# Merging four stages of a per-image pipeline into two software-pipelined loops, with one intermediate sent through DRAM

## The reference

```
x = gamma * (softmax(max(x x^T) - x x^T) x) + x        # channel attention: a 64 x 64 matrix per image
x = conv_long(x, filters of layer 1) + x * bias1       # 256-long causal filters along H and W
y = haar2d(x); for i in 0, 1: f = einsum(y * v[i], conv_w[i]); acc += sign(f) * relu(|f| - tau[i])
x = haar2d_inverse(acc) + x                            # wavelet shrinkage
x = conv_long(x, filters of layer 3) + x * bias3
```

## Time and profile before

| | before |
|---|---|
| median of 3 runs | 6840.18 us (6823.84 to 6842.23) |
| the profiled execution | 6835.24 us, of which the span from first to last instruction is 6833.4 us |
| TensorE clock granted, mean | 0.974 of full |
| PE busy | 6388.9 us |
| DVE / ACT / POOL busy | 4433.1 / 3968.3 / 2698.2 us |
| bytes over DMA | 944.27 MB |

### The profile page before, as it was taken

One profiled execution on the slowest core, in us unless ns is written; L12 is line 12 of the kernel. 1 busy time (PEld: TensorE's weight loads), 2 busy tenths in 40 slices (PEclk: granted clock), 3 DMA queues, 4 the chain that ended last, 5 costly groups with the idle time before them and its releaser, 6 DMA issues.

```text
span 6833.4 us, 144168 instructions
## 1 busy us (share of the span) xinstructions
PE 6388.9 (93%) x41056; PEld 5800.8 (85%) x41056; DVE 4433.1 (65%) x7037; ACT 3968.3 (58%) x5913; POOL 2698.2 (39%) x2052
## 2 busy tenths in 40 slices
PE   8998999889998899988999889998899988999689
PEld 7987999779997799977999779997799977998579
DVE  3667646676566764677646776567765677656766
ACT  1568545675456754567545775457654576545865
POOL 0149311483115831167311673117631176311852
PEclk9999999999999999999999999999999999999999
DMA  6654666546664466644666446664466644665236
GB/s 222 126 139 138 123 168 132 141 129 130 169 132 141 126 130 167 132 146 122 131 167 132 147 121 131 167 132 145 122 130 169 131 149 119 131 173 125 80 86 129
DMA packets 621293, 944.27 MB, mean 138 GB/s; under 512 B 62358, under 2 KB 456759, under 8 KB 621208
## 3 DMA queue, kind: packets, MB, share of 16 engines
q1 hardware_dynamic: 547480, 808.74, 51.3%
q10 hardware_dynamic: 73728, 134.25, 5.3%
HBM read 673.92 MB, written 268.83 MB: 138 GB/s over the span
## 4 chain that ended last, share of the span: by engine, by line
PE 75%; DVE 10%; ACT 8%; issue 3%; DMA 2%; POOL 1%; DVEq 1%; SPq 0%; ACTq 0%; POOLq 0%
PE ps L359 26%; PE ps L361 13%; PE ps L387 7%; PE ps L379 7%; PE ps L464 7%; PE ps L416 7%; PE ps L370 6%; DVE work L767 4%; DVE ps L782 4%; ACT ps L601 4%; ACT mag L598 4%; DMA work<-in_x_pix 1%; POOL mag L844 1%; PE ps L337 1%; DMA coef<-work 0%
## 5 line engine op out<-in xcount | busy, mean ns | idle before, releaser
L359 PE MATMUL ps<-work 128*128 128x256 f32 x8192 | 2455.2, 382 | 23.9 <-POOL work L833 16.3
L361 PEld LDWEIGHTS ps<-work 128*128 128x128 f32 x8192 | 1561.8, 191 | 214.3
L361 PE MATMUL ps<-work 128*128 128x128 f32 x8192 | 1578.0, 274 | 0.0
L359 PEld LDWEIGHTS ps<-work 128*128 128x128 f32 x8192 | 1315.8, 192 | 121.5 <-issue 20.7
L833 POOL COPY work<-field 128x512 f32 (+1 forms) x512 | 312.8, 614 | 2308.6 <-DVE ps L731 1623.3
L844 POOL TENSOR_TENSOR mag<-mag,sgn 128x1024 f32<-128x1024 f32 x512 | 1091.8, 2132 | 331.9 <-ACT mag L598 315.6
L862 POOL TENSOR_TENSOR split_a<-field,split_a 128x512 fp32r<-128x512 f32 x512 | 650.8, 1271 | 1418.8 <-ACT split_a L616 1418.8
L782 DVE TENSOR_TENSOR ps<-ps,tau_t 128x1024 f32<-128x1024 f32 x512 | 631.2, 1233 | 313.0 <-ACT ps L601 313.0
L569 ACT ACTIVATE work<-ps 128x512 f32<-128x512 f32 x512 | 306.1, 598 | 874.0 <-PE ps L361 871.1
L616 ACT ACTIVATE split_a<-field 128x512 fp32r (+1 forms) x512 | 322.9, 631 | 698.9 <-PE ps L379 694.6
L767 DVE TENSOR_TENSOR work<-ps,v_t 128x1024 f32<-128x1024 f32 x512 | 622.3, 1215 | 92.9 <-PE ps L464 92.9
(11 more groups left out here) (76 smaller groups left out, 9942.9 us busy)
## 6 DMA issues: line engine op xcount, KB each, us to landing
work<-filt SPq DMA_DIRECT2D x2048, 128.0 KB, 4.0
work<-in_x_pix SPq DMA_DIRECT2D x256, 512.0 KB, 5.4
coef<-work ACTq DMA_DIRECT2D x512, 256.0 KB, 2.1
out<-work SPq DMA_DIRECT2D x512, 256.0 KB, 4.1
rows<-in_x_rows SPq DMA_DIRECT2D x128, 512.0 KB, 4.4
mag<-in_x_rows SPq DMA_DIRECT2D x128, 512.0 KB, 4.4
rows<-coef SPq DMA_DIRECT2D x128, 512.0 KB, 3.6
split_a<-coef SPq DMA_DIRECT2D x64, 512.0 KB, 3.7
```

The lines of the kernel that those rows point to most:

```text
L359: nc.tensor.matmul(o_ps, src[:, 0, H * half:H * half + H], tab[:, N - 1::-1], start=True, stop=False)
L361: mm = nc.tensor.matmul(o_ps[:, H:N], src[:, 1, H * half:H * half + H], tab[:, N - 1:H - 1:-1], start=False, stop=True)
```

## The change

The kernel keeps three images in flight, each in another stage of work:

- `forward_stage(b)` runs, in one loop of 64 steps, the shrinkage of image b, the forward transforms of image b+1, and the Gram matrix of image b+2.
- `inverse_stage(b)` runs the inverse of image b and, in its 48 middle steps, the mix of image b+2: 64 slots, one or two ahead of a step's inverse work. `mix_w` is now the stationary operand, with 512 columns of `x` moving. ACT copies each result to `staged` and issues its store to a new DRAM tensor `mixed`; SP loads it back channel by channel into `img` in the forward stage. The copies of mixed data into `field` by DVE and ACT, and POOL's copies from `field` to `img`, are gone.
- Since both stages need PSUM at once, the 1,024 columns of a shrink unit become two halves of 512, in one PSUM bank each, with every operation on them issued twice. The Gram chunks are halved (512 KB).
- The split of the first Toeplitz result into high and low parts is gone: it is kept as fp32 in `x1`, and `haar_fwd` does four fp32 matmuls where it did eight fp32r ones.
- The first two mixes, the first forward and the last shrink have no partner: they run alone, by the same code.

```
-GP = 16
+GP = 8
...
+def mix_slots(j):
+
+    return [j + j // 3 + m for m in range(2 if j % 3 == 2 else 1)]
...
+def inverse_rounds(eng, lags, inv, mix, step):
+
+    if inv:
+        for j in range(8):
+            step(0, j, [lag <= j for lag in range(lags + 1)], None, [])
+
+    def steps(r):
+        for j in range(12):
+            step(3 * r + 2, j, [inv] * (lags + 1), r, mix_slots(j) if mix else [])
+
+    with eng.Fori(0, 3) as r:
+        steps(r)
+    steps(3)
+    if inv:
+        for j in range(8 + lags):
+            step(14, j, [j - lag < 8 for lag in range(lags + 1)], None, [])
...
+def timeline(eng, B, forward_stage, inverse_stage):
+
+    inverse_stage(-2, inv=False, mix=True)
+    forward_stage(-1, fwd=True, shrink=False, gram=True)
+    inverse_stage(-1, inv=False, mix=True)
+    with eng.Fori(0, B - 2) as b:
+        forward_stage(b, fwd=True, shrink=True, gram=True)
+        inverse_stage(b, inv=True, mix=True)
+    forward_stage(B - 2, fwd=True, shrink=True, gram=False)
+    inverse_stage(B - 2, inv=True, mix=False)
+    forward_stage(B - 1, fwd=False, shrink=True, gram=False)
+    inverse_stage(B - 1, inv=True, mix=False)
 
...
+        mixed = nc.dram_tensor("mixed", (C, H, 2 * N), F32, kind="Internal").ap()
...
+                    if fwd and not (isinstance(q, int) and q == 0):
+                        sp.wait_ge(f_x1, n - 3 + CR)
...
                         sp.wait_ge(f_mm2, n - 3 + CR)
                         sp.nop(nofuse=True)
-                        sp.dma_start(tab_a[:, d % 4, :], window(LY1, 4 * q + d)).then_inc(ftab_in[d % 4], 16)
-                        sp.dma_start(tab_b[:, d % 4, :], window(LX1, 4 * q + d)).then_inc(ftab_in[d % 4], 16)
...
+                        load_img(4 * q + j, j)
+                        fwd_tables(4 * q + j, j)
...
+                    if j % 2 and not (isinstance(q, int) and q == 0):
+                        if shrink:
+                            sp.wait_ge(c_copy, 64 * b + 4 * q + j - 3 + CR)
+                            sp.nop(nofuse=True)
+                            load_coef(b, 2 * q + j // 2, j // 2)
+                        if gram:
+                            load_pix(b + 2, 2 * q + j // 2, j // 2)
...
-                        for piece in range(2):
-                            mm = nc.tensor.matmul(o_ps, src[:, piece, kh, H * half:H * half + H], s_fwd[:, kh, :],
-                                                  start=(kh == 0 and piece == 0), stop=(kh == 1 and piece == 1),
-                                                  skip_group_check=True)
+                        mm = nc.tensor.matmul(o_ps, src[:, kh, H * half:H * half + H], s_fwd[:, kh, :].bitcast(F32),
...
+                        toeplitz(0, img[:, j], tab_a[:, j]).then_inc(f_mm1, 1)
...
+                        product(0)
+                    if gram and on[1]:
+                        gram_half(0)
...
+                        toeplitz(1, mid[:, d1 % 2], tab_b[:, d1 % 4]).then_inc(f_mm2, 1)
+                    if shrink and on[0]:
+                        product(1)
+                    if gram and on[1]:
+                        gram_half(1)
...
+                        haar_fwd(2, x1[:, j % 2]).then_inc(f_mm3, 1)
...
+                    if shrink and on[0]:
+                        turn()
...
+                        nc.tensor.matmul(ps[:, 6 + m % 2, :], mix_w[:, :],
+                                         xrows[chunk % 4][:, 512 * (m % 2):512 * (m % 2) + 512],
+                                         start=True, stop=True).then_inc(mix_mm, 1)
+
+                    for m in slots:
+                        mix_one(m)
...
+                    if fwd and on[4]:
+                        d = j - 4
                         act.wait_ge(f_res, n - 4 + 1 + CR)
                         act.nop(nofuse=True)
...
+                    if fwd and on[0]:
...
-                        nc.scalar.activation(mid[:, j % 2], ps[:, 0, :].rearrange("p (a n) -> p a n", a=2),
-                                             ACT.Copy).then_inc(f_mid, 1)
-                    if on[1]:
-                        d = j - 1
-                        act.wait_ge(f_x1, n + CR)
-                        act.wait_ge(f_mm3, n - 1 + CR)
-                        nc.scalar.activation(split_a[:, 0], ps[:, 1 + d % 2, :].rearrange("p (a n) -> p a n", a=2),
-                                             ACT.Copy).then_inc(f_x1hi, 1)
...
+                        nc.scalar.activation(mid[:, j % 2], halved(ps[:, 0, :]), ACT.Copy).then_inc(f_mid, 1)
+                    if shrink and on[0]:
+                        absolute(0)
+                        sign(0)
+                        relu(0)
+                        absolute(1)
+                        sign(1)
+                    if fwd and on[2]:
...
+                    if shrink and on[0]:
+                        relu(1)
+                    if fwd and on[3]:
...
+                    def mix_copy(m):
+                        act.wait_ge(mix_mm, 64 * g + 16 * r + m + 1 + CR)
+                        act.wait_ge(mixed_out[m % 2], 16 * (32 * g + 8 * r + m // 2) + 16)
+                        nc.scalar.activation(staged[:, m % 2], ps[:, 6 + m % 2, :], ACT.Copy).then_inc(mix_copied, 1)
+
+                    def mix_store(m):
+                        act.wait_ge(mix_copied, 64 * g + 16 * r + m + 1 + CR)
+                        act.nop(nofuse=True)
+                        rows_of = mixed.rearrange("c (s t) n -> (c s) (t n)", s=2)
+                        act.dma_start(rows_of[:, bass.ds(512 * (16 * r + m), 512)], staged[:, m % 2])\
+                            .then_inc(mixed_out[m % 2], 16)
...
+                    if shrink and on[0]:
+                        scale(0)
+                    if fwd and on[4]:
+                        d = j - 4
+                        mean, detail = res[0:1, d % 2, 0, :], res[0:1, d % 2, 1, :]
+                        dve.wait_ge(f_copied, n - 4 + 1 + CR)
+                        nc.vector.tensor_tensor(mean, mean, ps[0:1, 3, N:2 * N], ALU.add)
+                        nc.vector.tensor_tensor(detail, ps[0:1, 3, 0:N], detail, ALU.subtract).then_inc(f_res, 1)
+                    if shrink and on[0]:
+                        less(0)
+                    if shrink and on[1]:
...
-                        dve.wait_ge(f_x1hi, n + CR)
-                        dve.wait_ge(f_mm3, n - 1 + CR)
-                        nc.vector.tensor_tensor(split_a[:, 1], bank, split_a[:, 0].bitcast(F32), ALU.subtract)\
-                            .then_inc(f_x1lo, 1)
...
+                        dve.wait_ge(c_pair, u + CR)
+                        dve.wait_ge(c_copy, 64 * b + 4 * q + j + CR)
...
+                    if shrink and on[0]:
+                        scale(1)
+                    if fwd and on[1]:
+                        d = j - 1
+                        dve.wait_ge(f_mm2, n + CR)
+                        dve.wait_ge(f_mm3, n - 1 - 1 + CR)
+                        nc.vector.scalar_tensor_tensor(out=x1[:, d % 2], in0=img[:, d % 4],
+                                                       scalar=bias1[:, bass.ds(4 * q + d, 1)], in1=halved(ps[:, 1, :]),
+                                                       op0=ALU.mult, op1=ALU.add).then_inc(f_x1, 1)
+                    if shrink and on[0]:
+                        less(1)
+                    if fwd and on[2]:
+                        dve.wait_ge(f_hi, n - 1 + CR)
...
-                        nc.gpsimd.tensor_copy(img[:, j % 4],
-                                              field[:, :, bass.ds(4 * q + j, 1), :].rearrange("p a o n -> p (a o) n"))\
-                            .then_inc(f_img, 1)
...
+                    for a in range(2):
+                        u = 2 * (64 * b + 4 * q + j) + a
...
+                        nc.gpsimd.tensor_tensor(mag[:, a], mag[:, a], sgn[:, a], ALU.mult).then_inc(c_mult, 1)
                         pool.wait_ge(c_mult, u + 1 + CR)
-                        pool.wait_ge(c_field, u - 1 + CR)
-                        both = mag[:, d].rearrange("p (a i n) -> p a i n", a=2, i=2)
```

More of the change, by code:

```diff
@@ L65, in haar_signs, with quads @@
     return s, logs
-def quads(eng, count, lags, step, size=4):
-    for j in range(size):
+def quads(eng, count, lags, step):
+    for j in range(4):
         step(0, j, [lag <= j for lag in range(lags + 1)])
     with eng.Fori(1, count) as q:
-        for j in range(size):
+        for j in range(4):
             step(q, j, [True] * (lags + 1))
@@ L319, in _ @@
+            timeline(sp, B, forward_stage, inverse_stage)
             for s in y_out:
@@ new lines, in halved, with inverse_stage, step @@
+            def halved(t):
+                return t.rearrange("p (a n) -> p a n", a=2)
+            def inverse_stage(b, inv, mix):
+                g = b + 2
+                if mix:
+                    att_copy(g)
+                if not inv:
+                    att_rev(g)
+                    att_weights(g)
+                    att_place(g)
```

(4 more changed lines are left out.)

720 lines of the change are left out of this document (350 added, 370 removed).

## The result

The changed kernel takes 7304.82 us (median of 4 runs, 7287.54 to 7309.31), the kernel before in the same comparison 6833.11 (4 runs): the ratio is 1.0687, with a 95% interval from 1.067 to 1.0705. I had predicted 7010, with a range up to 7150. The direction was right, the size was not: 472 us slower, not 170.

A forecast was written before the change was run, and what follows sets the result against it. PE bounds every stage but shrink, a chain between engines; merged, such chains set the forward step. Merged images -132, unpartnered work +284, start +19 make +171 on 6835, 7006; the median lies 5 higher: 7010 us, range 6790 to 7150.

The forecast's parts named there:

- The inverse stage, the first forward, the start: Merged inverse 325 us against 330; first forward alone with Gram 320 us; smaller Gram chunks at the start +19 us.
- Two rounds through ACT and DVE set the merged step: Merged forward: a round without PE of 7.49 us and one through PE of 7.5 make the step 7.6 us.
- the twelve links: Merged forward: start-to-start links of the DVE and ACT round, summing to 7.49 us; step 8.0 if each is 0.04 longer.
- rival 3: Merged forward: coefficient loads arrive late, the step is 8.0 us, +180, total 7185 us; chance 0.15.
- One handover of 7 in a forward stage: Merged forward: 7 us (0 to 14) added to 64 steps of 7.6, making 493 us.
- Mixes alone, 1.65 a slot (1.5 to 1.9): First two mixes, without partner: 1.65 us a slot, 106 us each, 212 together.
- Rival 4: Mixes alone: stores land in 4 us, not 2.1, a slot takes 2.4, +96 for both, total 7105; chance 0.07.
- My other bound, 1.5 from the engines' rate: Mixes alone: the DMA engines need 1.5 us a slot, beside 1.45 from the staging buffer's round.
- The last shrink, 5.8 a step: Last shrink alone: 5.8 us a step (5.4 to 6.2), 380 us in all against 240.9 before.
- Rival 1: Merged forward: PE's 7.1 us sets the step, deciding from 7.22 down; total 6780 us (6740 to 6820); chance 0.14.

The follow-up runs named there:

- both runs on ACT's order: Changed kernel with the coefficient store issued after mid, absolute value and sign: 6862.3 us; the same with its wait for DVE's rows kept at the old place: 7150.6 us.
- the run with early pixels: Next Gram's pixels loaded ahead of an inverse stage's last outputs, next coefficient rows later, against the mended kernel with four buffers: 6742.5 us against 6742.0.
- both edits: Changed kernel with the late coefficient store issue and the coefficient load ahead of pixels and tables: 6837.1 us, 1.0008 of the kernel before.
- the other edits: Late store issue and early coefficient load; with the outer loop also written out 6802.5 us, against 6837.1 without.

## Why the prediction was right in direction and wrong in size

**The inverse stage, the first forward, the start** (325, 320, +19): right. The inverse took 325.6. The forward alone took 320 (263 to 583 us), and the first mix's first matmul moved from 103.6 to 120.2 us, +17.

**Two rounds through ACT and DVE set the merged step.** The mechanism was right, and both runs on ACT's order show it. The size was not: I had 7.6, measured were 8.04. It was mis-sized in two parts. The chain gives 7.77 in most steps and 7.85 on average where loads are early. Of the twelve links, the one across the store came out at 1.20 for 1.14, and the last at 0.82 for 0.60. The last is the meeting of the two rounds: the low part has ended at 1911.65, and the scaling starts at 1911.78, behind PE's product of 1910.52. I had treated them as two sums and added 0.1 for their meeting and for loop ends; it was 0.36. The other 0.19 are late coefficient rows, which was rival 3. I had it as another case with a chance of its own and a step of 8.0 in rounds of two steps; the rounds of two steps are there, on top of a longer chain. 0.44 us over 64 steps make 28 us an image, some 170 for six.

**One handover of 7 in a forward stage.** This failed. The forward windows are 534.4 long, of which 64 steps of 8.04 are 515, so 20 are left, 13 more than I had, some 80 for six. With the 28 of the steps that is the 41 us by which this stage is longer than 493. About 10 are the branch back over the body, shown by the loop written out. The rest is not settled: the waits for pixels and outputs stand there, but the run with early pixels put a wait for coefficient rows in their place. I had read 14 us as the worst from stages of the kernel before.

**Mixes alone, 1.65 a slot (1.5 to 1.9).** Wrong, by +55 for both: 2.1. The step that failed is the landing of 2.1 us, from the earlier trace rows. It is 3.1 in this stretch, with loads and stores at once. Rival 4 was this, with 2.4 a slot and 7 in 100, and I gave it so little because "the only store row" was 2.1. It was not the only one. The page of the kernel before has another store of 256 KB, which I overlooked:

```profile
out<-work SPq DMA_DIRECT2D x512, 256.0 KB, 4.1
```

Both were taken at nearly the same share of the DMA engines (0.61 and 0.62), so a landing can't be carried from one queue and place to another. The Trainium skill, "DMA: Bandwidth & Descriptors", Latency and other measured facts, has the access to DRAM at 0.2 us on average and 2 at high load. Within the mixes alone the trace agrees in direction, as the landing was 3.1 us at a share of 0.73 and 4.7 at 0.98. Over the kernel it does not follow the share. My other bound, 1.5 from the engines' rate, was met when four buffers took the wait for the landing out.

**The last shrink, 5.8 a step.** Right, 5.71. That two halves could be made to overlap by order alone, which I tried after it, was not so.

**Rival 1, PE sets the step (6780).** Refuted for the kernel as changed. It came true when the store was moved, with PE's step at 7.04 for the 7.1 of the sum (the four fp32 Haar matmuls take 0.82 us to the next instruction, 1906.67 to 1907.49, and the old eight took 0.93, so they cost nothing, as forecast), but the time with both edits was 6837, not 6780: the mixes and handovers kept their price. So no change lies at a step of about 7.04, and not at 7.22.

**Chances.** Slower was right at 0.77. The range was too narrow above since late loads and late landings stood as rivals of which one at most could be true, and the handover as a number without a spread. All three came short in the same direction, and they add. Whether they have one cause is not shown.

**What the structure is worth.** With ACT's order, SP's order, the loop and the buffers mended, the two merged loops take 6742 us, 0.9867 of the kernel before (0.985 to 0.9883). This is not the gain of the merging alone: with the loop kept and two buffers it was none (1.0008), and the kernel before, which stands still for 2.76 us between two images, was not run with its own loop written out. What is shown is that the order inside two engines' queues hid 467 us.

## What to carry to other kernels

When two jobs are merged on an in-order engine, look first at each wait of the old job on another engine, a store's wait for its data above all. It was harmless while nothing urgent stood behind it, and here it cost 442 us with the issue, of which the issue alone gave back 154; the cure was to move the store behind three operations. Price it with all the work queued behind it that then can't overlap (here `mid` and the absolute value), and with the loads that this work releases, and not with the duration of the stalled instruction. Look at single steps and not at their mean alone: here every second one had another limit. Rivals that can be true at the same time should be added to the forecast, not set against it.

## What the runs showed of the hardware

- After the branch back over the body of this outer loop PE stood still for 5.74 us with nothing to wait for, and the granted clock then was 0.50 for the next matmuls (0.64 us for one that takes 0.38) and 1.00 from 1600 us on. Writing the loop out won 50 us for 5 such branches, and 35 us with the other edits in place.
- The landing of a 256 KB store is not set by the mean share of the DMA engines. In the mixes alone it was 3.1 us at a share of 0.73 and 4.7 at 0.98. But in the kernel before, two stores took 2.1 and 4.1 at 0.61 and 0.62; and in the changed kernel the store of coefficients took 3.8 in a merged forward stage (0.63), and that of mixed rows 5.5 in a merged inverse (0.77).
- In a stage that never keeps PE busy, another order of the same instructions moved the mean granted clock from 0.81 to 0.69, and PE's busy time from 222.57 to 246.29 us. The better overlap on paper came with a longer step.
